# GpSimd computes the token's scale, VectorE its reciprocal behind the first product of gate and up

## The reference

```python
def fake_quant(t, axis):
    s = jnp.max(jnp.abs(t), axis=axis, keepdims=True) / QMAX
    s = jnp.maximum(s, 1e-08)
    q = jnp.clip(jnp.round(t / s), -QMAX - 1.0, QMAX) * s
    return t + jax.lax.stop_gradient(q - t)
...
gate = qlinear(x, w_gate)      # 512 -> 1376
up = qlinear(x, w_up)
h = jax.nn.silu(gate) * up
return qlinear(h, w_down)      # 1376 -> 512
...
x = x + _L0_ffn_ref(_L0_cond_ref(x, cond_128, ...), ...)
```

## Time and profile before

| | us |
|---|---|
| median of 3 runs | 304.40 |
| lowest and highest | 304.13, 304.82 |
| the profiled execution | 304.84 |
| its span in the trace | 303.1 |

### The profile page before, as it was taken

How to read it: one execution, slowest core, us unless ns; L and a number is a source line. 1 busy time by engine, 2 the same in 40 slices (tenths; PEclk the granted TensorE clock), 3 DMA queues, 4 the chain that set the end, 5 groups by cost and what they waited for, 6 DMA issues and landing times.

```text
span 303.1 us, 4742 instructions
## 1 busy us (share of the span) xinstructions
PE 286.7 (95%) x1629; PEld 168.5 (56%) x1629; DVE 250.7 (83%) x407; ACT 194.6 (64%) x229; POOL 199.3 (66%) x207
## 2 busy tenths in 40 slices
PE   7995788898999999999999999999999999999995
PEld 7995455475555555555444476656444444445443
DVE  3879469986999898888989868987988889889863
ACT  1265699987557777564788744544688867666640
POOL 1586659995657766554777854634787887666653
PEclk9999999999999999999999999999999999999999
DMA  7999703559995655544359984533355584343336
GB/s 273 416 422 351 294 11 76 130 130 284 293 359 67 170 134 149 139 118 89 100 153 288 224 220 120 77 90 97 94 151 152 154 197 119 82 93 109 82 91 214
DMA packets 80535, 51.59 MB, mean 170 GB/s; under 512 B 69536, under 2 KB 70048, under 8 KB 79616
## 3 DMA queue, kind: packets, MB, share of 16 engines
q1 hardware_dynamic: 80224, 51.10, 60.3%
q10 hardware_dynamic: 288, 0.20, 0.3%
HBM read 25.99 MB, written 8.39 MB: 113 GB/s over the span
## 4 chain that ended last, share of the span: by engine, by line
PE 56%; DVE 11%; DMA 8%; POOL 8%; ACT 7%; issue 6%; SPq 3%; DVEq 0%; POOLq 0%
PE bank L954 31%; PE bank L971 16%; PE bank L841 7%; DMA slab<-x_blocks 6%; POOL sg_mem L472 5%; DVE h_mem L744 3%; DVE h_max L750 3%; DVE sg_mem L734 3%; SPq L299 2%; ACT h_mem L581 1%; ACT sg_mem L576 1%; DMA xq_mem<-yq_mem 1%; ACT wgu_t L532 1%; DMA hq_mem<-hq_mem 1%; POOL xq_mem L451 1%
## 5 line engine op out<-in xcount | busy, mean ns | idle before, releaser
L472 POOL TENSOR_TENSOR sg_mem<-sg_mem,gu_scale_row 128x512 f32<-128x512 f32 (+1 forms) x96 | 111.3, 1162 | 78.2 <-ACT sg_mem L576 78.2
L954 PE MATMUL bank<-wgu_t,xq_mem 128*128 128x512 bf16 (+1 forms) x768 | 156.2, 357 | 6.0 <-DVE h_mem L744 4.3
L954 PEld LDWEIGHTS bank<-wgu_t,xq_mem 128*128 128x128 bf16 x768 | 73.7, 99 | 78.6 <-DVE h_mem L744 11.6
L576 ACT ACTIVATE sg_mem<-sg_mem,x_scale 128x512 f32<-128x512 f32 (+1 forms) x96 | 63.7, 674 | 49.5 <-DVE sg_mem L734 49.1
L971 PE MATMUL bank<-wd_t,hq_mem 128*128 128x512 bf16 (+1 forms) x341 | 78.2, 379 | 0.0
L734 DVE TENSOR_TENSOR sg_mem<-bank,gu_scale_row 128x512 f32<-128x512 f32 (+1 forms) x96 | 60.3, 628 | 20.1 <-PE bank L954 20.0
L744 DVE SCALAR_TENSOR_TENSOR h_mem<-bank,x_scale,sg_mem 128x512 f32<-128x512 f32 (+1 forms) x96 | 66.3, 692 | 10.6 <-POOL sg_mem L472 10.1
L581 ACT ACTIVATE h_mem<-h_mem,h_inv 128x1376 f32<-128x1376 f32 x32 | 46.1, 1442 | 30.6 <-DVE h_inv L626 30.6
L971 PEld LDWEIGHTS bank<-wd_t,hq_mem 128*128 128x128 bf16 (+1 forms) x341 | 33.3, 98 | 40.2 <-issue 0.3
L841 PEld LDWEIGHTS bank<-toeplitz,slab 128*128 128x128 f32 x320 | 48.3, 191 | 5.5 <-DMA slab<-x_blocks 2.0
L750 DVE TENSOR_REDUCE h_max<-h_mem 128x1 f32<-128x1376 f32 x32 | 50.5, 1578 | 0.0
(11 more groups left out here) (59 smaller groups left out, 132.5 us busy)
## 6 DMA issues: line engine op xcount, KB each, us to landing
xo_mem<-x SPq DMA_DIRECT2D x24, 256.0 KB, 2.9
out<-xo_mem SPq DMA_DIRECT2D x24, 256.0 KB, 2.1
slab<-x_blocks SPq DMA_DIRECT2D x3, 1088.0 KB, 6.1
hq_mem<-w_gate_up SPq DMA_DIRECT2D x6, 512.0 KB, 7.5
slab<-x_blocks SPq DMA_DIRECT2D x3, 1024.0 KB, 9.6
slab<-w_down SPq DMA_DIRECT2D x3, 688.0 KB, 9.1
h_mem<-w_gate_up SPq DMA_DIRECT2D x4, 512.0 KB, 14.3
slab<-x SPq DMA_DIRECT2D x1, 2048.0 KB, 9.7
```

What stands on the lines that cost most here:

```text
L472: pool.tensor_tensor(s, s, gu_scale_row[:, 1, at:at + n], ALU.mult).then_inc(silu_scaled, 1)
L576: act.activation(s, s, ACT.Silu, scale=x_scale[:, i:i + 1]).then_inc(silu_done, 1)
L954: last = pe.matmul(bank[n % 2][:, 0:cols], xq_t[:, g, k, P * c:P * (c + 1)], wgu_t[:, m, k, at:at + cols], start=(k == 0), stop=(k == KT - 1))
```

## The change

The scale of a token leaves VectorE. It is computed by GpSimd, in a new function `token_scale` that stands between the residual addition and the second silu piece of the next tile; it waits for the maximum. The reciprocal stays on VectorE in a function of its own, `token_inverse`, and stands behind the next tile's first product of gate and up. The last tile's scale stands ahead of the five residual additions that follow GpSimd's loop. Values and their number are the same.

```diff
+            def token_scale(i):
+                one = slice(i, i + 1)
+                pool.wait_ge(h_max_ready, i + 1)
+                pool.tensor_scalar(h_scale[:, one], h_max[:, one], 1.0 / QMAX, SMALLEST_SCALE, ALU.mult, ALU.max)\
+                    .then_inc(h_scale_ready, 1)
...
                 scale_silu(i, 0)
                 if i >= LAG + 1:
                     add_residual(i - LAG - 1)
+                if i:
+                    token_scale(i - 1)
                 scale_silu(i, 1)
...
+            token_scale(TILES - 1)
             for i in range(TILES - LAG - 1, TILES - 1):
                 add_residual(i)
...
-                scale_of(h_max[:, one], h_scale[:, one], h_max_ready, h_scale_ready, i + 1)
+
+            def token_inverse(i):
+                one = slice(i, i + 1)
                 inverse_of(h_scale[:, one], h_inv[:, one], h_scale_ready, h_inv_ready, i + 1)
...
                 multiply_up(i, 0)
+                if i:
+                    token_inverse(i - 1)
                 if i == 0:
...
             token_scales(TILES - 1)
+            token_inverse(TILES - 1)
             for i in range(TILES - LAG, TILES - 1):
                 scale_down(i)
```

## The result

The changed kernel takes 313.65 us in the median of 4 runs (312.53 to 313.76), against 304.61 (304.13 to 304.94) before. The ratio is 1.0277, with a 95% interval of 1.025 to 1.0304. The profiled execution took 313.58 us with a span of 311.4, against 304.84 and 303.1: 8.3 us more in the span and 0.44 more outside it. The 0.44 goes with the kernel and not with the execution: time less span is 2.2 us in every execution of the changed kernel and of experiments 2, 3 and 8, and 1.7 to 1.9 in every one of the kernel before and of the other six. Experiment 4 is among the six and also has all scales on GpSimd, so that is not enough to cause it; what does stays open.

What follows compares the result with a forecast made beforehand. TensorE, 95% busy at 7.03 us a tile, was taken as the bound, other engines barely keeping pace. Terms 1.8 + 2.4 + 3.8 + 0.6 = 8.6 us on the 304.4 median gave 313.0 us, range 309 to 316.

Steps and rivals of the forecast that it cites:

- the ring: Tile-to-tile loop through residual addition, scale, reciprocal and rounding: 8.08 us a turn against 7.02 before and TensorE's 7.03.
- The price of the scale: A 128x1 scale on GpSimd, read from the slope of wide tiles: 0.19 us, range 0.10 to 0.29.
- The product 0.41 us earlier: With the scale off VectorE, the first gate-up product can start 0.41 us earlier where its silu piece is there.
- The run 13 to 16: Tiles with two roundings of y and no convolution; TensorE was to lose 2.4 us there.
- the slack: Time a bank is free before TensorE's second gate piece needs it: 0.83 us in tile 16, 0.52 in tile 25.
- The run 21 to 24: Second run of tiles with two roundings of y and no convolution; TensorE was to lose 3.8 us.
- The first lag: Lateness from a run's first tile: 0.35 us for tile 21, before 1.06 a tile is added.
- The start: Tiles 1 to 6, bound by GpSimd and ScalarE in turns: TensorE's bound stretch entered 1.8 us later.
- The tail: Last tile: reciprocal 0.24 us late by the way over GpSimd, tile arriving 0.35 late; 0.6 us.
- the dear scale: Rival: the scale on GpSimd takes 0.62 us, as long as the 512-column form; 319 us, chance 0.05.
- The earlier product: Rival: TensorE's waits for the first product shrink, about 1.6 us together, giving 302.8 us; chance 0.05.
- everything is covered: Rival: late reciprocals meet idle time and the ring stays under 7.03; within 0.6 us of 304.4, chance 0.04.

Runs made afterwards that it cites:

- experiment 2: Against the kernel before: scale on GpSimd behind the residual addition, as in the change, but the reciprocal stays ahead of the first product; 321.88 us, ratio 1.0559.
- experiment 3: The changed kernel with the scale ahead of the residual addition in GpSimd's queue; 308.6 us, ratio 1.0115.
- experiment 8: The changed kernel with the scale ahead of the residual addition and that addition behind the second silu piece; 307.95 us, ratio 1.0107.
- Experiment 4: The changed kernel with the scale computed twice on GpSimd, the first time into a spare column; 315.75 us, ratio 1.0353.
- experiment 5: Against the kernel before: the change applied for the scales of tiles 0 to 5 alone; 305.91 us, ratio 1.0034.
- experiment 1: The changed kernel with the scale back on VectorE behind the reduction, the reciprocal still behind the first product; 308.13 us, ratio 1.0106.
- experiment 6: Against the kernel before: the change applied for the scales of tiles 21 to 24 alone; 308.5 us, ratio 1.0123.
- experiment 7: Against the kernel before: in turns 5, 13 and 21 the first product goes ahead of scale and reciprocal, both on VectorE; 304.8 us, ratio 1.0002.
- experiment 9: The kernel before with the residual addition moved behind the second silu piece, nothing else; 304.05 us, ratio 0.9984.

## Why the prediction was right

The mechanism held: the scale behind the residual addition makes the ring longer than TensorE's tile where y is rounded and no convolution stands beside it, and nowhere else. The sizes, term by term:

- **The price of the scale.** 0.19 predicted from the slope of wide tiles; 0.18 to 0.19 from start to start, measured by doubling. Right.
- **The product 0.41 us earlier.** In tile 21 of the changed kernel it comes 219.10 - 217.61 = 1.49 us behind the reduction's start, as worked out, and TensorE's wait falls from 0.68 to 0.25. In tile 22 and on, the product waits for the silu piece (0.75 us) and gains nothing. Right.
- **The ring.** 8.08 predicted, 8.10 to 8.11 measured, through the residual addition, the scale, the reciprocal and the rounding. Experiments 2 and 3 show the links: without the addition ahead 7.34, with the reciprocal ahead of the product 8.56. It is hidden with a convolution in the tile, and without roundings of y (6.8 to 7.0, predicted 6.86). Right.
- **The run 13 to 16.** 2.4 predicted, 2.44 measured. Right against the kernel before as traced. Both numbers rest on the 0.36 by which tile 14 was held there: with the slack of 0.53 from experiment 5 the same sum is 2.47 + 0.81 - 0.53 = 2.75.
- **The run 21 to 24.** 3.8 predicted, 3.86 measured, and 3.58 alone. The first lag plus three turns is there, and TensorE's last wait is for the third gate piece, as I had it: that piece starts at 253.32, 4.37 late on the run's entry, and 4.37 - 0.52 = 3.85. But the sentence that the second silu piece is late "with nobody close behind it" is wrong. The second product starts at 253.91, 3.82 late, and with 0.02 of slack that door gives 3.80. The two doors agree here to 0.05 us, which is luck and not something that I had worked out. In experiments 1 and 3 they differ by 0.43 and 0.74, and the step left out made those expectations too low.
- **The start.** 1.8 predicted, 1.64 at the milestone and 1.66 from tile 0's reduction. Alone it is 1.54 and 1.79, and 1.1 in the medians. The walk is weaker than this looks: for experiment 1 it gave 1.2, and 2.14 came. The reciprocal of tile 2 starts at 56.50, predicted 56.4, with the product ahead of it at 55.83.
- **The tail.** 0.6 predicted, 0.34 in the row. The reciprocal starts 1.92 us behind its reduction's start, and 1.81 before (289.20 to 291.01), so the way over GpSimd costs 0.11 where I had 0.24. The hop to GpSimd is 0.08 and not 0.14, the scale and the hop back 0.25 and not 0.32. The same 1.92 and 1.81 stand in experiments 2, 3 and 8 and in 1, 5, 6, 7 and 9. The tile's own lateness is as predicted: the reduction is 8.24 late against 7.94 of the run before, 0.30 for my 0.35. Of these 0.41, 0.07 are lost again before the last product. As a step of the milestones the 0.34 is not clear of what the tail moves by from trace to trace: experiments 3 and 8, with the same tail code, show +0.09 and -0.05.

The last tile's rows, in the timeline of the changed kernel:

```profile
297.44 1.59 DVE L759 TENSOR_REDUCE h_max<-h_mem 128x1 f32<-128x1376 f32 x1
299.11 0.21 POOL L477 TENSOR_SCALAR h_scale<-h_max 128x1 f32<-128x1 f32 x1 [2.43 <-DVE h_max L759]
...
299.36 0.17 DVE L635 RECIPROCAL h_inv<-h_scale 128x1 f32<-128x1 f32 x1 [0.34 <-POOL h_scale L477]
```

The sum in the span was 8.6, measured 8.3. That the total still came out at 313.65 against 313.0 owes something to luck: 0.44 outside the span, which I had not foreseen, made up for the smaller sum, and another 0.3 is the distance of the profiled pair from the medians. Of the rivals, the dear scale fell by its price. The earlier product fell by the ring, and experiment 7 adds that even without the late scale its gain does not last where the ring follows closely. That everything is covered fell by the ring.

## What to carry to other kernels

Before a small operation is moved to another engine, write down what stands ahead of it in that engine's queue and close the loop: which instruction of the next tile waits for its result, and how long one turn then takes against the pace of the engine that bounds. Here the operation cost 0.19 us and the 1.24 us instruction ahead of it made a hidden wait the bound in seven tiles (14 to 16 and 22 to 25). For the slack, walk every buffer that the bounding engine takes back in a turn, and not only the one that the ring names: three doors had 0.16, 0.52 and 0.02 us. And a wait removed at one place was a lasting gain here only where what feeds the next tile had time to spare. Last, compare two traces from a point ahead of the first change: here the same code differed by up to 2 us before it.

## What the runs showed of the hardware

**TensorE's clock fell in some executions, and in the changed kernel that cost nothing that shows.** In tile 2 of the changed kernel TensorE waited 2.28 us for the first product (1.46 before), and from 58 to 61 us the granted clock was 0.50, the lower level, and 1.00 again from 62 on. The timeline there:

```profile
56.64 5.05 PE L968 MATMUL bank<-wgu_t,xq_mem 128*128 128x352 bf16 x16 [2.28 <-DVE h_mem L753]
...
58.32 0.15 PEld L968 LDWEIGHTS bank<-wgu_t,xq_mem 128*128 128x128 bf16 x1 [0.28 <-issue]
...
58.75 0.15 PEld L968 LDWEIGHTS bank<-wgu_t,xq_mem 128*128 128x128 bf16 x1 [0.27 <-issue]
```

The weight loads are 0.43 us apart, 512 columns at 1.2 GHz, and the 16 matmuls take 5.05 us where they took 3.36. The wait alone does not decide it: in experiments 1, 2, 3 and 8 the clock fell at the same place behind waits of 2.08 to 2.29 us, and in experiments 4 and 5 it stayed at 1.00 behind 2.47 and 2.29. So the fall that I had expected in experiment 5 did not come. It gives the comparison: with the first six scales moved as well and the full clock, experiment 5 takes +1.79 from tile 0's reduction to the first milestone, and the changed kernel +1.66. The other executions of the changed kernel agree: at mean clocks of 0.993, 0.999, 0.995 and 0.999 the spans are 311.4, 311.5, 310.3 and 311.5. In experiment 6 it was not so: at 0.993 the span was 309.6, at 0.999 it was 306.7. There the clock was 0.83 between 25 and 35 us, ahead of the first tile, and tile 0's reduction started 1.97 us later than before; another 0.9 came in the tail.

**A small operation crosses cheaply.** The scale takes 0.216 us on GpSimd and 0.15 on VectorE. From its start to that of the reciprocal are 0.25 us over GpSimd (228.01, 228.26) and 0.19 in VectorE's own queue before (153.06, 153.25 in tile 14). With the way there it is 0.11 us in the tail, both crossings and the longer operation together. I had taken the full 0.13 of a wide piece's signal for the way back, and the row shows 0.03 behind the recorded end.

**Left open.** Why VectorE held the product for 0.32 us in tile 21 of experiment 1 and for 0.36 in tile 14 of the kernel before; why experiment 1 lost 2.14 us in the start; what brings 0.44 us outside the span in four of the kernels; and what decides whether the clock falls in tile 2.
